# Cross-attention over 16 heads and a routed expert layer on one core: the logits move from VectorE and GpSimd to TensorE, and q, k, v travel as one record

## The chip, the cores and the metric

The kernel runs on 1 core of one Trainium2 chip. The metric is the device time of one execution in microseconds (us), taken as the median of several runs; lower is better.

## The reference

x and ctx hold 32 tiles of 128 tokens by 256 channels, in float32. The attention has 16 heads of 16 channels, and it runs over the heads of one token's q, k and v (a 16x16 table of logits for each token), not over tokens:

```python
query = (layernorm(x) @ Wq.T + bq).reshape(B, -1, H, D)      # H = D = 16
key_p = (ctx @ Wk.T + bk).reshape(B, -1, H, D)
value = (ctx @ Wv.T + bv).reshape(B, -1, H, D)
logits = einsum('bsid,bsjd->bsij', query, key_p) / sqrt(D)
out = einsum('bsij,bsjd->bsid', softmax(logits), value)
x = x + transpose(out, (0, 2, 1, 3)).reshape(B, -1, O) @ Wd.T + bd
h = layernorm(x)
gates = softmax((h @ w_red) @ normalised(wg).T); idx = argmax(gates); score = max(gates)
x = x + score * (gelu(h @ W1[idx] + b1[idx]) @ W2[idx] + b2[idx])
```

The einsum sum runs over `i, j` of one token `s`; the transpose mixes the tokens of a tile afterwards. Each token goes to one of 8 experts.

## The kernel before, in words

All five engines run hand-ordered programs that meet at semaphores. A loop index t goes from 0 to LAST; in step t each engine works on several tiles at different stages, each `live` for 32 values of t.

**Attention (t = 0 to about 36).** SyncE loads x and ctx (`sync_attention`, L238). ScalarE takes mean and variance (`moments`, L689), GpSimd raises the variance to the power -0.5 (L359), ScalarE applies it (L723), TensorE transposes and projects k and v (L864) and q (L878); biases are added by bf16 matmuls against a row of ones (L868, L875, L919). The logits are products and sums outside TensorE: `qk_mult` (L204) multiplies q by k for 16x16x16 elements of each token, 12 of the 16 rows on GpSimd in two instructions and 4 on VectorE; `qk_sum` (L212) is two reduces of 2048 elements on VectorE into PSUM. VectorE subtracts the maximum (L496, L498), ScalarE exponentiates in PSUM (L784), VectorE normalises (L467, L469, L473; its table `pr` is in PSUM). The table goes through DRAM (`a_scr`) to be laid out as blocks `aexp`, v goes through DRAM (`v_scr`) to `v2`, both in pieces of 64 bytes, and TensorE multiplies them in 16 column-tiled matmuls (L891). Then Wd and, by a matmul with the identity, x (L922, L923), the second layernorm, two transposes and the gate (L944).

**Routing.** When the first R1 = 24 tiles have their gates, `vector_early` (L516, in four parts from t = NT on) computes for them which token goes to which slot of 128 rows of one expert; S1 = 17 slots come from it. `vector_late` (L580) does the rest beside the expert work.

**Experts (39 slots).** For each slot GpSimd gathers 128 rows by an indirect DMA and scatters the result (`pool_ffn`, L376), VectorE copies the expert's W1 (`vector_up`, L663), TensorE does 4x2 and 4 accumulating matmuls, each issued as two (L995, L1020), ScalarE applies Gelu (L804), VectorE adds bias, score and residual (`vector_down`, L684). Slots 0 to 6 are issued in steps t = NT+2 = 34 to 40 beside the end of the attention, the rest in a loop of their own.

What sets the order is the written order of each engine's program: an instruction that waits holds everything behind it on its engine. In VectorE's step (L451) it is: gate maximum, 4 rows of the product, sum and normalisation of an older tile, the two reduces, maximum, subtraction.

Of the kernel before, what the change touches and what calls it, by code (L numbers as in the profile page):

```python
# [4 lines left out]
P = 128  # L5
# [12 lines left out]
ROW = 2 * C + 4  # L18
BW = 4 * C
EPS = 1e-5  # L20
HALF = NH // 2
W1W = KC * HID + KH
NB = P // NH
POOLH = 12
XR = 10
CR = 5
LAGS = 8
# [4 lines left out]
R1 = 24  # L32
WORDER = (1, 2, 0, 3)
# [5 lines left out]
LAST = NT + LAGS  # L39
FIRST = NT + 2  # L40
WARM = {NT: 4, NT + 1: 22, NT + 2: 6, NT + 3: 6}
# [4 lines left out]
SEMS = ("ld_b ld_x0 ld_x1 ld_c0 ld_c1 st_v0 st_v1 ld_v0 ld_v1 st_a0 st_a1 ld_a0 ld_a1 st_r0 st_r1 st_r2 st_r3 st_r4 ld_w0 ld_w1 ld_w2 "  # L46
        "ld_w3 ld_g ld_b1 st_b ld_br ld_moe ld_b2 pad0 bsplit filled zeroed ident ones iotas const nmax gpow wrt wrTs b1T "
        "gmm gate cat0 bpart wtr wT gsq nr2 wide xn tr_in tr_c xT cT qq kv qcp kcp vcp qk0 qk1 qks qkred0 qkred1 mx lsub "
        "exp sm rsm norm pvo oT wd x2 x2n tr_g x2T glg gm gsub score "
        "nm0 nm1 va0 va1 ve0 ve1 rs nb0 nb1 oh cnt rv selr selp selk invmm texp idg ids ig isc yo yb "  # L50
        "oh_a cnt_a rv_a selr_a selp_a selk_a invmm_a texp_a idg_a gexp8 score8 st_s "
# [3 lines left out]
def live(t):  # L55
    return 0 <= t < NT
# [6 lines left out]
def build(nc, x, ctx_in, Wq, bq, Wk, bk, Wv, bv, Wd, bd, w_red, wg, W1, b1, W2, b2, out):  # L63
# [3 lines left out]
    a_scr = nc.dram_tensor("a_scr", [NT // 2, NB, 2, NH, NH, NH], f32, kind="Internal").ap()  # L67
    v_scr = nc.dram_tensor("v_scr", [NT, P, C], f32, kind="Internal").ap()
    row_scr = nc.dram_tensor("row_scr", [NTOK, ROW], f32, kind="Internal").ap()
    bias_scr = nc.dram_tensor("bias_scr", [3, BW], bf16, kind="Internal").ap()  # L70

    es = ExitStack()
    with es:
# [9 lines left out]
        wT = sb("wT", [P, KC, 4 * C])  # L83
        brow = sb("brow", [3, BW], bf16)
        ones = sb("ones", [P, P], bf16)
        ident = sb("ident", [P, P])
        gate = sb("gate", [P, KC, NE])
# [15 lines left out]
        sc8 = sb("sc8", [P, NT - R1])  # L103
        xt = sb("xt", [P, XR, C])
# [27 lines left out]
        bT, bQ, bKV, bO, bY, bG = (bank(n) for n in ("bT", "bQ", "bKV", "bO", "bY", "bG"))  # L132
        bL = [bank("bL0"), bank("bL1")]
        wbank = (bO, bKV, bL[0], bL[1])
        lg = [t[:, 0:C].rearrange("p (i j) -> p i j", i=NH) for t in bL]
        pr = [t[:, C:2 * C].rearrange("p (i j) -> p i j", i=NH) for t in bL]

        wst = [prod[1][:, KC * w:KC * (w + 1), :] for w in range(4)]
        NR = BW // P
        bst, bres, bres2 = (sb(n, [NR, P]) for n in ("bst", "bres", "bres2"))  # L140
        bsp = sb("bsp", [NR, 3, P], bf16)
        wrp, wrT = (b2b[:, k * C:(k + 1) * C].rearrange("p (a c) -> p a c", a=KC) for k in range(2))
        wgT = sb("wgT", [NG, NE])
        wgb, wgs = (b2b[:, 2 * C + k * P:2 * C + (k + 1) * P] for k in range(2))
# [4 lines left out]
        def fl(t):  # L149
            return t[:, :, :].rearrange("p a b -> p (a b)")  # L150

        r0, r1, x0, x1 = fl(prod[0]), fl(prod[1]), fl(aexp[0]), fl(aexp[1])
# [15 lines left out]
        selr_a = [r0[:, 768 * k:768 * (k + 1)].bitcast(bf16).rearrange("p (r n) -> p r n", r=P) for k in range(2)]  # L168
# [5 lines left out]
        pos_a, limv_a, bad_a, far_a = (early(3400 + 24 * k, R1) for k in range(4))  # L174
        pint_a, pir_a, pik_a = (early(3496 + 24 * k, R1).bitcast(i32) for k in range(3))
# [4 lines left out]
        selk = [x0[:, 2048 + 640 * k:2688 + 640 * k].bitcast(bf16)[:, 0:3 * S2P * NH2]  # L180
# [18 lines left out]
        yb = [r0[:, RB * ROW + YR * C:RB * ROW + (YR + 1) * C], r1[:, 3592:3592 + C]]  # L199
        held = sb("held", [P, 2])  # L200
        rsc = [sb(f"rsc{k}", [P, 1])[:, :] for k in range(2)]
        bH = [bKV, bL[0]]

        def qk_mult(eng, t, lo, hi, q_):  # L204
            return eng.tensor_tensor(  # L205
# [32 lines left out]
        def sync_attention(eng):  # L238
            for t in range(LAST + 1):
# [33 lines left out]
                if live(e) and e % 2 == 1:  # L273
                    n = e // 2
                    for k in range(2):
                        eng.wait_ge(S[f"st_a{k}"], (n + 1) * 16)
# [812 lines left out]
```

## Time and profile before

| what | value |
|---|---|
| median of 3 runs | 472.84 us (471.21 to 474.26) |
| the profiled execution | 472.96 us, span from first to last instruction 471.1 us |
| mean granted TensorE clock | 0.964 of full speed |
| busy: TensorE, VectorE, ScalarE, GpSimd | 428.2, 359.8, 282.0, 364.7 us |

The span is 1.9 us shorter than the execution's own time. Busy time is the time in which at least one instruction of the engine is running; the groups below give the mean of one instruction, which can overlap its neighbour, so the step from one start to the next is what an engine really spends.

### The profile page before, as it was taken

How to read it: one execution, taken by the hardware profiler on the slowest of the kernel's cores; microseconds unless marked ns; L12 is line 12 of the kernel's file. 1: busy time of each engine (PE TensorE's matmuls, PEld its weight loads, DVE VectorE, ACT ScalarE, POOL GpSimd, SP SyncE). 2: the span in 40 equal slices, each digit the busy share in tenths (PEclk: the TensorE clock that was granted, in tenths of full speed). 3: DMA queues.
4: the chain of work that ended last, by engine and by line, in shares of the span. 5: the costliest groups of instructions: out<-in, count | busy, mean ns of one | idle time of the engine just before them, and what ended most of it. 6: DMA issues, size and time to landing. Idle time of an engine off the chain costs nothing.

```text
span 471.1 us, 10138 instructions
## 1 busy us (share of the span) xinstructions
PE 428.2 (91%) x3093; PEld 313.5 (67%) x3093; DVE 359.8 (76%) x583; ACT 282.0 (60%) x978; POOL 364.7 (77%) x369
## 2 busy tenths in 40 slices
PE   7877999999999999999998689798899999999990
PEld 6544555656656565656565355687799999999980
DVE  4997999999999999999999971237884565555540
ACT  4554689999999999999996324725121233322220
POOL 6999999999999999999999103345594867777731
PEclk9987999999999999999999788989999999999997
DMA  5898674787587767867666539423332333333300
GB/s 143 271 392 267 123 107 73 154 152 148 93 158 164 133 102 147 166 142 117 132 111 110 83 52 180 152 78 92 66 115 64 108 108 114 102 101 95 101 28 0
DMA packets 170283, 59.40 MB, mean 126 GB/s; under 512 B 138761, under 2 KB 160434, under 8 KB 170102
## 3 DMA queue, kind: packets, MB, share of 16 engines
q1 hardware_dynamic: 165222, 44.24, 44.5%
q0 software_dynamic: 4992, 14.51, 10.6%
q8 instruction: 26, 0.43, 0.4%
q14 instruction: 27, 0.22, 0.2%
q10 hardware_dynamic: 16, 0.00, 0.0%
HBM read 37.68 MB, written 21.96 MB: 127 GB/s over the span
## 4 chain that ended last, share of the span: by engine, by line
DVE 48%; PE 38%; issue 7%; ACT 2%; POOL 2%; DMA 1%; DVEq 1%; SPq 0%; POOLq 0%; ACTq 0%
DVE bL L213 28%; PE bQ L1020 13%; PE bKV L995 7%; DVE prod L205 7%; PE bL L995 7%; DVE mx L496 3%; DVE sm L467 2%; PE bKV L864 2%; DVE rsm L469 2%; PE bT L1004 2%; PE bQ L878 1%; DMA prod<-in_L_xattn_Wv 1%; DVE gm L460 1%; PE bO L979 1%; PE bY L922 1%
## 5 line engine op out<-in xcount | busy, mean ns | idle before, releaser
L205 POOL TENSOR_TENSOR prod<-q,kk 128x2048 f32<-128x2048 f32 x64 | 218.7, 3441 | 0.9 <-ACT q L772 0.7
L213 DVE TENSOR_REDUCE bL<-prod 128x128 f32<-128x2048 f32 x64 | 143.3, 2284 | 0.0
L1020 PE MATMUL bQ<-w,prod 128*128 x312 | 74.6, 382 | 2.9 <-DVE prod L679 2.9
L1020 PEld LDWEIGHTS bQ<-w,prod 128*128 128x128 f32 x312 | 56.3, 191 | 10.9 <-issue 4.8
L864 PE MATMUL bKV<-wT,xcT 128*128 128x512 f32 x128 | 62.6, 613 | 0.0
L804 ACT ACTIVATE prod<-bKV,prod 128x128 f32<-128x128 f32 x80 | 22.8, 368 | 56.8 <-PE bKV L995 56.8
L411 POOL DMA_INDIRECT out<-prod,isc x39 | 39.8, 1021 | 21.1 <-issue 21.1
L804 ACT ACTIVATE prod<-bL,prod 128x128 f32<-128x128 f32 x76 | 21.6, 367 | 44.5 <-PE bL L995 44.5
L359 POOL TENSOR_TENSOR rs<-ve,half 128x2 f32<-128x2 f32 x39 | 28.4, 728 | 24.5 <-ACT ve L698 22.5
L404 POOL DMA_INDIRECT prod<-row_scr,ig x39 | 40.2, 1030 | 5.8 <-issue 2.2
L679 DVE TENSOR_TENSOR prod<-bQ,b2b 128x256 f32<-128x256 f32 x39 | 16.5, 423 | 34.4 <-PE bQ L1020 33.9
L205 DVE TENSOR_TENSOR prod<-bQ,kk 128x1024 f32<-128x1024 f32 x32 | 38.9, 1214 | 3.4 <-ACT q L772 3.3
L995 PEld LDWEIGHTS bKV<-prod 128*128 128x128 f32 x320 | 39.5, 196 | 1.2 <-issue 0.4
L922 PE MATMUL bY<-wT,oT 128*128 128x256 f32 x128 | 37.9, 420 | 2.6 <-ACT oT L777 2.6
L995 PE MATMUL bKV<-prod 128*128 128x128 f32 x320 | 40.2, 280 | 0.0
L995 PEld LDWEIGHTS bL<-prod 128*128 128x128 f32 x304 | 36.6, 192 | 2.9 <-issue 2.1
L995 PE MATMUL bL<-prod 128*128 128x128 f32 x304 | 37.2, 276 | 1.2 <-DVE prod L668 1.2
L891 PE MATMUL bO<-aexp,v 128*32 128x128 f32 x1024 | 35.4, 280 | 2.9 <-DMA aexp<-a_scr 2.9
L663 DVE TENSOR_SCALAR prod<-w1b 128x1028 f32 x39 | 27.6, 707 | 13.2 <-issue 11.8
L878 PE MATMUL bQ<-wT,xcT 128*128 128x256 f32 x128 | 37.1, 413 | 0.0
L864 PEld LDWEIGHTS bKV<-wT,xcT 128*128 128x128 f32 x128 | 22.5, 196 | 16.0 <-issue 16.0
L410 POOL TENSOR_TENSOR held<-half 128x1 f32<-128x1 f32 x39 | 9.2, 237 | 30.0 <-DVE prod L684 29.8
(214 smaller groups left out, 799.6 us busy)
## 6 DMA issues: line engine op xcount, KB each, us to landing
row_scr<-cat SPq DMA_DIRECT2D x32, 258.0 KB, 4.4
xt<-in_x SPq DMA_DIRECT2D x16, 256.0 KB, 3.5
ct<-in_ctx SPq DMA_DIRECT2D x16, 256.0 KB, 3.7
v_scr<-vs SPq DMA_DIRECT2D x32, 128.0 KB, 3.0
w1b<-in_L_ffn_W SPq DMA_DIRECT2D x8, 512.0 KB, 8.7
w<-in_L_ffn_W SPq DMA_DIRECT2D x8, 512.0 KB, 8.6
a_scr<-a SPq DMA_DIRECT2D x32, 128.0 KB
v<-v_scr SPq DMA_DIRECT2D x32, 128.0 KB, 3.9
```

The lines of the kernel that those rows point to most:

```text
L205: return eng.tensor_tensor(prod[t % 2][:, lo:hi, :].rearrange("p i (j d) -> p i j d", j=NH), q_[:, lo * HD:hi * HD].rearrange("p (i d) -> ...
L213: return eng.tensor_reduce(lg[t % 2][:, h * HALF:(h + 1) * HALF, :], prod[t % 2][:, h * HALF:(h + 1) * HALF, :] .rearrange("p i (j d) -> p ...
L359: eng.tensor_tensor(rs[:, :], ve[:, :], half2[:, :], ALU.pow).then_inc(S["rs"], 1)
L404: eng.indirect_dma_start(gr[k], None, row_scr[0:R1 * P] if a < S1 else row_scr, bass.IndirectOffsetOnAxis(ap=ig[k][:, :], axis=0)).then_in ...
L411: eng.indirect_dma_start(out, bass.IndirectOffsetOnAxis(ap=isc[k][:, :], axis=0), yo[k], None, bounds_check=NTOK - 1, oob_is_err=False).th ...
L804: i_ = eng.activation(hT[a % 2][:, k, :], bH[a % 2][:, k * P:(k + 1) * P], ACT.Gelu, bias=w1s[a % 2][:, KC * HID + k:KC * HID + k + 1])
L864: eng.matmul(bKV[:, :], xcT[:, KC + k, :], wT[:, k, C:3 * C], start=(k == 0), stop=False)
L878: i_ = eng.matmul(bQ[:, 0:C], xcT[:, k, :], wT[:, k, 0:C], start=False, stop=(k == KC - 1))
L891: i_ = eng.matmul(bO[32 * r:32 * (r + 1), m * P:(m + 1) * P], v2[c % 2][:, 32 * l - 16 * s:32 * l - 16 * s + 32], aexp[c // 2 % 2][:, c % ...
L922: eng.matmul(bY[:, 0:C], oT[:, k, :], wT[:, k, 3 * C:4 * C], start=False, stop=False)
L995: i_ = eng.matmul(bH[a % 2][:, k * P:(k + 1) * P], w1s[a % 2][:, c * HID + k * P:c * HID + (k + 1) * P], gT[a % 2][:, c, :], start=(c == 0 ...
L1020: i_ = eng.matmul(bQ[:, 0:C], hT[b % 2][:, k, :], w2[:, bass.ds(eb * (KH * C) + k * C, C)], start=(k == 0), stop=(k == KH - 1))
```

## The change

The logits are now made on TensorE. VectorE writes q, k and v with their biases into one record of 16x48 floats a token, (`qkv`), which is stored to `qkv_scr` (393 KB a tile) and loaded back by heads (`ql`, in pieces of 192 bytes). GpSimd expands k to 16 blocks of 128 columns with a mask of zeros (`kx`, 2048 elements), ScalarE copies q and v into padded form (`pad`), and 16 column-tiled matmuls give the logits. The softmax table is normalised in SBUF (`pr` is now an SBUF tile), transposed by TensorE, and expanded by VectorE with the same mask (`ax`, 2048 elements). The gate's weights are multiplied into Wq and Wd in the setup, so gate logits come as 8 more columns of both projections. x is added by VectorE, bd by GpSimd. R1 is 20 and `vector_early` is in seven parts at t = 25 to 31, beside full attention steps; slots start at t = 31. The weights of the experts are loaded one transfer a step (t = 2 to 17) where before 16 transfers were issued in t = 1 and 2. The scores of the last five tiles are exponentiated after the attention loop.

```diff
-R1 = 24
+R1 = 20
-LAST = NT + LAGS
-FIRST = NT + 2
+LAST = NT + 6
+FIRST = NT - 1
+ROUTE = R1 + 5
-EXPERTS_IN = {1: range(0, NE // 2), 2: range(NE // 2, NE)}
+EXPERTS_IN = 2
...
 def pool_attention(eng):
-    for t in range(LAST + 1):
-        a, v, d = t, t - 1, t - 7
+    for t in range(-1, LAST + 1):
+        a, n, d, z = t, t + 1, t - 6, t - 2
...
+            eng.tensor_tensor(rs[t % 3][:, :], ve[:, :], half3[:, :], ALU.pow).then_inc(S["pw"], 1)
+            eng.wait_ge(S["pw"], t + 2)
+            eng.tensor_tensor(nb[t % 3][:, :], nm[:, :], rs[t % 3][:, 0:2], ALU.mult).then_inc(S["rs"], 1)
...
+        if live(z):
...
+            eng.wait_ge(S[f"ld_q{z % 2}"], (z // 2 + 1) * 16)
...
+            eng.tensor_tensor(block(kx[:, z % 2, :]), spread_heads(ql[z % 2][:, :, 0:HD]), mask_b,
+                              ALU.mult).then_inc(S["kx"], 1)
+        if live(a):
...
+            eng.tensor_tensor(xt[:, a % XR, 0:C], xt[:, a % XR, 0:C], bdb[:, :], ALU.add).then_inc(S["xb"], 1)
...
 def vector_attention(eng):
     for t in range(LAST + 1):
+        a, s0, s1, w = t, t - 3, t - 4, t - 5
...
+            # tile s0: maximum and subtraction in bL, after wait qk
+            # tile w:  cat = bY + xt (264 columns), then gate maximum
...
+            eng.tensor_tensor(block(ax[:, :]), spread_heads(bA[:, 0:C].rearrange("p (l i) -> p l i", l=NH)),
+                              mask_b, ALU.mult).then_inc(S["ax"], 1)
...
+            for k in range(2):
+                i_ = eng.tensor_tensor(qkv[a % 2][:, :, 2 * k * HD:(2 * k + 1) * HD], heads(bKV[:, k * C:(k + 1) * C], k),
+                                       heads(bqkv[:, k, :], k), ALU.add)
...
+            eng.tensor_tensor(qkv[a % 2][:, :, HD:2 * HD], heads(bQ[:, 0:C], 0), heads(bqkv[:, 2, :], 0), ALU.add)
...
+            eng.scalar_tensor_tensor(xt[:, a % XR, C:EXT], bQ[:, C:EXT], rs[(a - 1) % 3][:, 2:3], bdg[:, :],
+                                     ALU.mult, ALU.add).then_inc(S["qad"], 1)
...
+            # tile s0: sum, reciprocal, a2 = pr * rsm (both in SBUF)
+        if ROUTE <= t < ROUTE + 6:
+            vector_early(eng, t - ROUTE)
...
 def tensor_attention(eng):
...
+    # order of a step: tr_in(t) | logits blocks(t-3) | Wd(t-5), 264 columns | transpose a2(t-4)
+    #   | k,v(t), 512 columns | q(t), 264 columns | value blocks(t-4) | tr_c(t+1)
```

(The comment lines stand for code that is told here in short.) ScalarE's step is: copy of the transposed x (t), the `pad` copy (t-2, waits for the load), second layernorm and score (t-6), first layernorm (t+1), exponent (t-3), gate shift and moments (t-5), moments (t+2), copy of the values (t-4), copy of the transposed ctx (t+1). The 512 columns for k, v, the waits of each buffer and the expert slots' functions are otherwise as before.

## Rows read from the trace of the kernel before

**Rows 1.** The page: busy time of each engine, and the chain that ended last.

```profile
PE 428.2 (91%) x3093; PEld 313.5 (67%) x3093; DVE 359.8 (76%) x583; ACT 282.0 (60%) x978; POOL 364.7 (77%) x369
...
DVE 48%; PE 38%; issue 7%; ACT 2%; POOL 2%; DMA 1%; DVEq 1%; SPq 0%; POOLq 0%; ACTq 0%
```

**Rows 2.** Windows (busy PE, PEld, DVE, ACT, POOL, then clock, DMA share, GB/s).

```profile
140.00:180.00 40.00, 38.95 (x301) 23.86 (x301) 38.86 (x48) 37.37 (x136) 39.20 (x16) 1.00 0.74 141
265.00:280.00 15.00, 12.33 (x115) 7.79 (x116) 13.96 (x39) 4.54 (x16) 0.70 (x1) 0.84 0.35 57
350.00:400.00 50.00, 50.00 (x354) 47.45 (x353) 29.05 (x73) 14.02 (x50) 33.99 (x74) 1.00 0.33 98
```

**Rows 3.** Timeline of a full attention step: start us, us, engine, line, what.

```profile
160.30 0.70 POOL L359 TENSOR_TENSOR rs<-ve,half 128x2 f32<-128x2 f32 x1 [0.17 <-ACT ve L698]
160.33 0.42 DVE L496 TENSOR_REDUCE mx<-bL 128x16 f32<-128x256 f32 x1
160.48 0.44 PE L833 MATMUL bT<-ident,ct 128*128 128x128 f32 x2
...
160.78 0.43 DVE L498 TENSOR_TENSOR bL<-bL,mx 128x256 f32<-128x256 f32 x1
...
160.97 6.84 POOL L205 TENSOR_TENSOR prod<-q,kk 128x2048 f32<-128x2048 f32 x2
...
161.13 0.15 DVE L460 TENSOR_REDUCE gm<-bG 128x1 f32<-128x8 f32 x1
161.20 1.21 DVE L205 TENSOR_TENSOR prod<-bQ,kk 128x1024 f32<-128x1024 f32 x1
...
162.33 0.41 DVE L467 TENSOR_REDUCE sm<-bL 128x16 f32<-128x256 f32 x1
...
163.48 4.48 DVE L213 TENSOR_REDUCE bL<-prod 128x128 f32<-128x2048 f32 x2
163.48 1.88 PE L864 MATMUL bKV<-wT,xcT 128*128 128x512 f32 x4
163.68 0.38 ACT L744 ACTIVATE x2T<-bG 128x256 f32<-128x256 f32 x1 [0.20 <-PE bG L855]
...
165.40 0.29 ACT L698 ACTIVATE ve<-va,eps 128x1 f32<-128x1 f32 x1
...
167.13 1.08 PE L891 MATMUL bO<-aexp,v 128*32 128x128 f32 x32
```

**Rows 4.** Groups by shape, 100 to 230 us: busy, mean ns of one.

```profile
L205 POOL TENSOR_TENSOR prod<-q,kk 128x2048 f32<-128x2048 f32 x18 | 81.3, 4518 | 0.0
L922 PE MATMUL bY<-wT,oT 128*128 128x256 f32 x69 | 19.7, 406 | 0.0
L723 ACT ACTIVATE xn<-xt,nb,rs 128x256 f32<-128x256 f32 x17 | 10.2, 601 | 0.0
L692 ACT ACTIVATE junk<-xt 128x256 f32<-128x256 f32 x17 | 7.1, 418 | 0.0
```

**Rows 5.** DMA issues: KB each, median us to landing.

```profile
row_scr<-cat SPq DMA_DIRECT2D x32, 258.0 KB, 4.4
...
v_scr<-vs SPq DMA_DIRECT2D x32, 128.0 KB, 3.0
...
v<-v_scr SPq DMA_DIRECT2D x32, 128.0 KB, 3.9
```

**Rows 6.** Timeline: VectorE and GpSimd instructions that met.

```profile
9.09 3.50 POOL L340 MEMSET aexp<- 128x4096 f32 x1
...
10.10 3.57 DVE L438 CAST io_r<-io_r 128x2048 bf16<-128x2048 f32 x1
...
331.24 0.62 DVE L610 TENSOR_TENSOR aexp<-aexp,oh 128x256 f32<-128x256 f32 x1
331.33 0.58 POOL L392 COPY ig<-idg 128x1 int32<-128x1 int32 x1
```

**Rows 7.** Timeline: GpSimd's wait for the routing, and the first and last result slots.

```profile
281.25 0.19 POOL L392 COPY ig<-idg 128x1 int32<-128x1 int32 x1 [14.94 <-DVE idg L577]
...
304.92 0.48 DVE L684 SCALAR_TENSOR_TENSOR prod<-prod,rsc 128x256 f32<-128x256 f32 x1
...
460.63 0.48 DVE L684 SCALAR_TENSOR_TENSOR prod<-prod,rsc 128x256 f32<-128x256 f32 x1
...
462.00 1.00 POOL L411 DMA_INDIRECT out<-prod,isc  x1 [0.54 <-issue]
```

More of the change, by code:

```diff
@@ L615, in vector_late @@
[L615 to L623 removed]
+                after(eng.tensor_scalar(rnd, pos, (1.0 - P) / 2, ROUND, ALU.add, ALU.add))
@@ new lines, in tensor_attention @@
+                if live(a):
+                    if a > 0:
+                        eng.wait_ge(S["kvad"], a)
+                    else:
+                        eng.wait_ge(S["wT"], 2)
+                    for k in range(KC):
+                        i_ = eng.matmul(bKV[:, :], xcT[:, KC + k, :], wT[:, k, 0:2 * C], start=(k == 0),
+                                        stop=(k == KC - 1))
+                    i_.then_inc(S["kv"], 1)
+                    if a > 0:
+                        eng.wait_ge(S["qad"], a)
@@ L924, in tensor_attention @@
-                if live(d) and not live(a):
-                    tensor_gate(eng, d)
-                if t < 5:
-                    fill(eng, 10, bO)
-                if t == NT:
-                    eng.wait_ge(S["vcp"], NT)
-                    eng.wait_ge(S["wide"], 1)
-                for _ in range(WARM.get(t, 0)):
-                    eng.matmul(bKV[:, :], ones[:, :], io_r[:, 0:32, :].rearrange("p r n -> p (r n)"),
-                               start=True, stop=True)
-                if t == NT:
+                    tensor_down(eng, s)
@@ new lines, in tensor_attention @@
+                if live(s1):
+                    eng.wait_ge(S["ax"], s1 + 1)
+                    if s1 > 0:
+                        eng.wait_ge(S["oT"], s1)
+                    blocks(eng, bO, pad[:, s1 % 3, 2 * C:4 * C], ax[:, :]).then_inc(S["pvo"], 1)
+                if live(a + 1):
+                    tensor_context(eng, a + 1)
+                for s in slots:
+                    tensor_rows(eng, s)
+                if t < 4:
+                    fill(eng, 10, bA)
+                if t == ROUTE:
@@ L1025, in build @@
         rv_a, rv = [0], [0]
-        block = es.enter_context(nc.Block())
-        @block.sync
+        engines = es.enter_context(nc.Block())
+        @engines.sync
         def _(eng):
@@ L1032, in _ @@
             sync_attention(eng)
-        @block.gpsimd
+        @engines.gpsimd
         def _(eng):
@@ L1040, in _ @@
             pool_end(eng)
-        @block.vector
+        @engines.vector
         def _(eng):
@@ L1056, in _ @@
                 scalar_ffn(eng, s)
-        @block.tensor
+        @engines.tensor
         def _(eng):
```

887 lines of the change are left out of this document (413 added, 474 removed).

## The prediction

> **What bounds the kernel now.** I read the page's busy line and chain first [rows 1]: the chain is VectorE for 48% and TensorE for 38%, so there are two stages. The windows [rows 2] part them: from 140 to 180 us VectorE is busy 38.86 and GpSimd 39.20 of 40 us; from 350 to 400 us TensorE is busy all 50. Between them, 265 to 280, GpSimd works 0.70 of 15 us: it waits 14.94 us for the routing [rows 7].
> In a full attention step [rows 3] VectorE never pauses: maximum at 160.33, subtraction at 160.78 (0.45 later), gate maximum 161.13, product 161.20, sum 162.33 (1.13 later), reduces from 163.48 for 4.48 us, next maximum at 167.99. The step is 7.66 us, and 32 of them are the first stage. GpSimd is nearly as full: 6.84 for two products, 0.7 for the power. The last stage is 155.7 us from slot 0's result (304.92) to slot 38's (460.63), then 10.5 us to the end of the span [rows 7]; the diff leaves its work per slot alone.
>
> **The new attention step, engine by engine** (start to start, from [rows 3, 4]).
> VectorE loses the two reduces (4.48) and the 1024-element product (1.13). It gains the expansion, 2048 elements: the 1024-element product's step is 1.13, of which 0.07 is fixed (161.13 to 161.20 for a tiny one), so 2.20; four adds of some 256 elements at 0.35 (the step behind the subtraction) and one of 8 at 0.1. With maximum 0.45, subtraction 0.35, residual add and gate maximum 0.46+0.07, sum, reciprocal and a2 0.45+0.36+0.34: I take one residual add, three adds into the record, and get 5.8 us. Call M the start of the maximum; the expansion starts at M+1.33, the record is ready at M+4.7, a2 starts at M+5.5 and ends at M+5.9.
> GpSimd: power 0.70, a small multiply about 0.2, k's expansion 4.52 (the same 2048 elements of two inputs [rows 4]; bounds 4.5 and, were it at the pair's 6.84 for 3072 elements, 4.6), bd about 0.74 (a quarter of 2.1 us per 1024 plus 0.2). Sum 6.2.
> TensorE: three pairs of transposes at 0.37, k and v 1.71, q and Wd 0.89 each (four matmuls of 264 columns, 0.216 of step each), two sets of blocks at 1.01 (L891, from 167.13 to the next start). Sum 6.6. It drops the bias rows, the identity matmul and the gate's four. But the ctx transposes, now last in the step, must be copied by ScalarE before the next step's transposes may start. A copy starts 0.47 after its transposes do (163.21 to 163.68), takes 0.38, and 0.08 leads back: 0.94 in place of 0.37. TensorE's loop is 7.17 us. The loop through the logits, VectorE and the value blocks is as long: 0.37+1.16+1.33+2.28+0.05+1.01+0.94 = 7.14.
> ScalarE: two moments of 1.45 (a 0.418 activation, its accumulator, a second pair, ve), two layernorm applications 0.51 each, copies at 0.29, the pad copy of 512 elements 0.56 (bounds 0.5 and 1.0: once or twice L723's 0.51), scores 0.5; with its own wait for TensorE 6.9 us.
> DMA: M is 1.5 us into the step (0.37+1.16), so the record is ready at 6.2. The store of 393 KB is bounded by 3.0 and 6.6 (128 KB took 3.0, 258 KB 4.4 [rows 5]; one and a half times the latter); I take 4.7, as fixed latency is a large part of it. The load, 2048 pieces of 192 bytes, is bounded by 3.9 (as many pieces of 64) and 6; I take 4.7. It lands 15.7 us after (with 0.1 for the issue) its step began, and `pad` wants it two steps on. From there ScalarE's rest of the step is 6.2: three steps in 15.7+6.2 = 21.9 us, 7.3 each. So four resources lie between 6.9 and 7.3; I take 7.3 (bounds 6.9 and 7.9), 0.36 less than 7.66.
>
> **Where the two elementwise engines meet.** A rival price is inside the profile [rows 6]: VectorE's cast began at 10.10 while GpSimd's memset ran from 9.09 to 12.59, and lasted to 13.67, where 2048 elements need about 1.1 after 12.59. And GpSimd's copy of one element, begun 0.09 after a VectorE multiply with both inputs in SBUF, took 0.58 in place of 0.19 and ended 0.05 after it. So the two wait for each other for a whole instruction. In the kernel before, every VectorE instruction beside the 6.8 us of GpSimd products has a PSUM input. After the change a2 reads two SBUF tiles, and so do most of the routing's instructions, which now stand in steps 25 to 30 beside k's expansion. The Trainium skill, "SBUF — State Buffer", section "Who interferes with whom", says the same: a VectorE instruction with two SBUF inputs and a GpSimd one that reads SBUF exclude each other, and the later one blocks fully. The trace agrees (0.58 against 0.19); without that rule and those rows the forecast would be the first rival's.
> When does k's expansion start? The power waits for ScalarE's moments: exponent at M+0.92 at the earliest, shift M+1.45, moments of 1.47 twice, to M+4.6, then 0.1+0.78+0.2: M+5.66, not 0.2 after a2 has started. In a normal step the load lands later (rel. M+6.8). So a2 passes first, and the plain steps pay nothing.
> Routing: its parts take 1.1 to 2.1 us each by the same instructions of the kernel before and follow a2. Part 0 (step 25) fits before k's expansion. The other five meet it: from M+5.9 VectorE stands until M+10.3, then finishes 1.4 to 2.1 us of routing: 12.1 us a step in place of 7.3. Without exclusion such a step would be 5.8+2 = 7.8.
>
> **The sum.** Record 0 is ready at 13.5 (setup as long as before: k, v of tile 0 at about 11), stored 18.0, loaded 22.7, expanded 27.4, its logits at 28.6 = M of step 3. Then 23 steps of 7.3: 196.5 = M of step 26. Five steps of 12.1: 257. Step 30 ends with 20 small matmuls of the inversion which wait for the last selection, in front of the next step's transposes: +2, 259. Steps 31 and 32: no q, k, v work, but GpSimd's power now waits for one moment only, so k's expansion starts at M+4.2, before a2, and holds it to M+8.7; with the first W1 copy 9.1 and 10.6. Step 33, 7.0; result of slot 0 some 6.5 into step 34: 292.2. In the kernel before this was 304.92, of which 15 us were GpSimd's wait; that wait goes. From there the stage of 39 slots as before, 155.7, and 10.5: span 458.4, and with 1.9 outside it 460.3 us, against 472.96 of the profiled execution and the median 472.84, which are the same within 0.1%. Saved are some 7 us in plain steps and 26 between step 31 and the first result (33 in place of 59, by the step of 7.66 counted back from the last one); some 26 are paid back in steps 26 to 30, and the rest is in the first steps, where the weights' transfers no longer stand in one block.
> Costed at nothing: the setup's products with Wq and Wd (TensorE waits for weights there; uncovered, 2 us), the weights' transfers in steps 2 to 17 (the DMA share was 0.74 with 4096 pieces of 64 bytes a tile, now 2048; uncovered, about 1 us a step, 16 us), the table loads between Gelu and exponent (1.3 us each, hidden under TensorE). The granted clock is 1.00 in a full step and 0.84 from 265 to 280 us [rows 2], where TensorE was busy 12.3 of 15. In the blocked steps TensorE has 6.6 us of work at full clock in 12; at the lower level it would still fit.
>
> **The rivals.**
> 1. No exclusion in the routing steps, since the routing's instructions pass between. For it: part 0 does. Against: rows 6, and 4.5 us of expansion in each step. Steps of 7.8: 22 less; steps 31 and 32 5 less: 434 us. Chance 0.22.
> 2. The exclusion locks in. If k's expansion starts before a2 in plain steps too (0.2 us decide, at M+5.66 against M+5.5), a2 ends 4.5 later and the next step starts so: 10.6 us a step. ScalarE is then ahead, so it repeats itself. 22 plain steps of 3.3 more: 533 us. For it: any long step brings the load in early. Against: the order at the margin, and that the load is late in plain steps. Chance 0.10, slower.
> 3. The trip through DRAM is longer, 12 us and more beside the weights' transfers: steps of 8.1 to 8.3, 478 to 483 us. For it: a store of 393 KB, twice the 64-byte pieces' bytes. Chance 0.10.
> The forecast has 0.58.
>
> **How the numbers follow.** The forecast's own spread is 9 us (0.4 on 23 steps). The measurement can tell about 1% from no change. Below 468.1 lie 0.85 of the forecast and rival 1: 0.70 for faster. Within 1%: 0.08 of the forecast and a little of rival 3, 0.10. Slower 0.20. The range, 431 to 484, takes in rivals 1 and 3 and leaves out the lock.
>
> **What would show it.** Attention steps of 7.3 us with VectorE busy under 6 of them; a2 at its plain 0.4 us in plain steps; in steps 26 to 30 a routing instruction with a duration of 3 to 4.5 us beside k's expansion, and steps of 12 us; first slot's result near 292; 3.73 us a slot at the end. Wrong it is if a2 lasts over 4 us in plain steps (rival 2), if no routing instruction is long (rival 1), or if GpSimd and ScalarE wait for the load for over 1 us a step (rival 3).

## The result, and the profile after

The changed kernel takes 494.12 us (median of 4 runs, 493.2 to 498.86) against 473.55 us for the kernel before (471.21 to 475.87) in the same comparison: a ratio of 1.0455, 95% interval 1.0368 to 1.0541. It is slower. The forecast was 460 us, with 431 to 484 as its range; the result lies outside. The prediction's own rival 2 (chance 0.10) is there, in a milder form, but it is not the whole of it: of the 34 us between forecast and measurement it holds about 10, and without it the kernel is still slower than before (e1, e2). The profiled execution has a span of 493.0 us.

I read the page first: busy line, chain, three groups and three transfers (columns of the groups: engine, operation, tiles, count, busy us, mean ns, idle before).

```profile
PE 404.7 (82%) x3785; PEld 308.1 (62%) x3785; DVE 351.2 (71%) x664; ACT 253.3 (51%) x835; POOL 302.2 (61%) x407
...
PE 40%; DVE 24%; DMA 16%; issue 11%; ACT 5%; SPq 2%; DVEq 1%; POOL 0%; ACTq 0%; POOLq 0%
...
L344 POOL TENSOR_TENSOR kx<-ql,mask 128x2048 f32<-128x2048 f32 x32 | 117.5, 3673 | 25.9 <-issue 22.8
L329 POOL TENSOR_TENSOR rs<-ve,half 128x3 f32<-128x3 f32 x39 | 34.8, 892 | 90.6 <-ACT ve L682 90.6
...
L492 DVE TENSOR_TENSOR a<-pr,rsm 128x256 f32<-128x256 f32 x32 | 56.5, 1766 | 3.6 <-DVE rsm L488 0.5
...
qkv_scr<-qkv SPq DMA_DIRECT2D x32, 384.0 KB, 3.9
ql<-qkv_scr SPq DMA_DIRECT2D x32, 384.0 KB, 4.7
```

Against [rows 1] GpSimd and VectorE gave up 62.5 and 8.6 us of busy time, and the kernel still got slower. The chain, which was VectorE for 48% and TensorE for 38%, now has 16% DMA: the wait for the record is visible in it. The row to stop at is a2 (L492): 32 instructions of 256 elements with a mean of 1766 ns, where the same form takes 590 ns when nothing holds it (the timelines below). A mean of this kind hides two populations, so I looked at stretches and at single steps. The windows (busy PE, PEld, DVE, ACT, POOL, then clock, DMA share, GB/s):

```profile
84.00:145.00 61.00, 54.45 (x657) 35.14 (x656) 50.33 (x97) 49.15 (x169) 43.34 (x33) 1.00 0.89 240
190.00:226.00 36.00, 23.44 (x285) 14.36 (x283) 35.24 (x44) 21.99 (x73) 21.70 (x16) 1.00 0.51 141
221.00:226.00 5.00, 0.57 (x10) 0.20 (x2) 4.86 (x5) 0.72 (x2) 4.92 (x4) 0.99 0.50 164
226.00:231.00 5.00, 3.40 (x37) 2.37 (x38) 1.78 (x5) 2.17 (x7) 0.65 (x1) 0.50 0.34 47
360.00:480.00 120.00, 119.10 (x810) 111.99 (x809) 67.85 (x163) 34.30 (x120) 79.69 (x176) 0.97 0.32 92
```

From 84 to 145 us VectorE is busy for 50.33 of 61 us, the DMA engines for 0.89 (0.74 in [rows 2]). From 190 to 226 us VectorE is busy 35.24 of 36 again, though no work was added and the DMA load has fallen. The slot stage (360 to 480) is as it was. The granted clock is 1.00 from 190 to 226 us, so TensorE's clock does not lengthen these steps. I call a step locked when a2 stands in it until k's expansion is through. One such step, 206.88 to 216.46, in the timeline (start us, us, engine, line, what):

```profile
211.41 0.86 POOL L329 TENSOR_TENSOR rs<-ve,half 128x3 f32<-128x3 f32 x1 [3.91 <-ACT ve L682]
...
212.50 3.67 POOL L344 TENSOR_TENSOR kx<-ql,mask 128x2048 f32<-128x2048 f32 x1
212.66 3.88 DVE L492 TENSOR_TENSOR a<-pr,rsm 128x256 f32<-128x256 f32 x1
...
216.46 0.41 DVE L435 TENSOR_REDUCE mx<-bL 128x16 f32<-128x256 f32 x1
...
216.59 0.44 PE L858 MATMUL bA<-ident,a 128*128 128x128 f32 x2 [1.60 <-DVE a L492]
...
217.37 0.38 ACT L735 ACTIVATE pr<-bL 128x256 f32<-128x256 f32 x1 [2.03 <-DVE bL L437]
...
219.99 0.91 DVE L464 TENSOR_TENSOR qkv<-bKV,bqkv 128x256 f32<-128x256 f32 x2
...
220.82 0.58 DVE L475 TENSOR_TENSOR qkv<-bQ,bqkv 128x256 f32<-128x256 f32 x1
...
221.32 0.22 DVE L479 SCALAR_TENSOR_TENSOR xt<-bQ,rs,bdg 128x8 f32<-128x8 f32 x1
```

k's expansion starts 0.16 before a2, and a2 ends 0.37 after it. The next maximum, TensorE's transposes of a2 (1.60 idle) and ScalarE's exponent (2.03 idle) all wait for that one instruction. Then GpSimd waits 3.91 for ScalarE and both meet again 9.58 us later, 222.08 against 222.25. Nothing pulls them apart: the late a2 delays everything by the same amount. In the routing steps of this kernel the instruction that is held is again a2 (3.86 to 3.88 us in steps 26 to 29, for example at 237.74), and none of the routing's own, which run behind it and take 1.30 us at most:

```profile
237.74 3.88 DVE L492 TENSOR_TENSOR a<-pr,rsm 128x256 f32<-128x256 f32 x1
```

In a plain step under the weights' transfers the order is the other one, since the record has not landed (idle before k's expansion 1.97, and `pad` shows what it is: the load):

```profile
119.86 0.59 DVE L492 TENSOR_TENSOR a<-pr,rsm 128x256 f32<-128x256 f32 x1
...
121.66 0.63 ACT L708 ACTIVATE pad<-ql 128x512 f32<-128x512 f32 x1 [1.14 <-DMA ql<-qkv_scr]
121.71 3.68 POOL L344 TENSOR_TENSOR kx<-ql,mask 128x2048 f32<-128x2048 f32 x1 [1.97 <-issue]
```

The starts of the maximum (M) divide the loss. "M of 3" is the start in step 3, "3->20" the time from step 3's to step 20's, all in us and each from one profiled execution; the last column runs from M of step 31 to the last slot's result.

```
                      M of 3   3->20   20->25  25->26  26->31  M of 31  31->last slot
predicted               28.6   124.1     36.5     7.3    62.5    259.0     188.9
after                  36.07   131.5     48.9    14.2    61.0    291.6     190.8
after, once more       36.68   136.0     48.5    14.2    60.8    296.2     191.1
e1 rsm in PSUM         37.09   137.2     38.4    13.9    57.9    284.4     190.6
e2 wait for a2         37.90   137.5     40.6    13.8    62.5    292.4     186.3
e3 waits a2, routing   35.60   135.8     41.1     9.7    44.3    266.5     185.0
e4 weights spread only 36.84   150.9     48.3    14.2    60.8    311.2     189.4
e5 e3, weights spread  36.16   128.2     39.1    10.3    43.3    257.1     187.0
e6 setup               34.89   125.0     41.7     9.7    43.0    254.3     186.5
e7 order of TensorE    35.38   123.9     36.5    10.1    44.4    250.2     186.7
e8 rsm in PSUM again   33.92   123.8     42.1     9.7    43.0    252.5     192.6
e9 bias table only     37.28   139.6     47.9    14.2    60.4    299.5     188.2
e10 bias table late    35.93   121.5     34.8     9.7    43.1    245.0     186.4
```

Of 32.6 us at step 31, 7.5 are the start, 7.4 plain steps, 12.4 lie between steps 20 and 25 (four locked steps of 9.6 to 10.2, and before them one of 9.9, which is not locked: the bias table's transfer lies in it, e10), and 6.9 in the step from 25 to 26, the first routing step; the five steps behind it came out at 61.0 where 62.5 were forecast. Another 1.9 us are lost behind step 31. The four locked steps hold 9.8 us more than four of 7.3.

### The profile page after: what moved, and what is told of

The parts are those of the page before. It is cut to its first block, busy times and chain, and to the rows that moved or that the text cites. A ratio compares the mean times of both kernels' runs of the same rounds, so it can differ in the third digit from the quotient of the medians.

```text
span 493.0 us, 11383 instructions
## 1 busy us (share of the span) xinstructions
PE 404.7 (82%) x3785; PEld 308.1 (62%) x3785; DVE 351.2 (71%) x664; ACT 253.3 (51%) x835; POOL 302.2 (61%) x407
## 3 DMA queue, kind: packets, MB, share of 16 engines
q0 software_dynamic: 4992, 14.61, 10.2%
## 4 chain that ended last, share of the span: by engine, by line
PE 40%; DVE 24%; DMA 16%; issue 11%; ACT 5%; SPq 2%; DVEq 1%; POOL 0%; ACTq 0%; POOLq 0%
PE bQ L995 13%; DMA qkv_scr<-qkv 9%; DVE a L492 7%; PE bKV L962 7%; PE bX L962 6%; DMA ql<-qkv_scr 5%; PE bY L851 3%; PE bL L822 3%; DVE ax L455 3%; DVE qkv L464 2%; DVE cat L444 2%; PE bT L977 2%; DMA bdc<-in_L_xattn_bd 1%; SPq L256 1%; DVE qkv L475 1%
## 5 line engine op out<-in xcount | busy, mean ns | idle before, releaser
L344 POOL TENSOR_TENSOR kx<-ql,mask 128x2048 f32<-128x2048 f32 x32 | 117.5, 3673 | 25.9 <-issue 22.8
L995 PE MATMUL bQ<-w,wA 128*128 x312 | 74.6, 382 | 3.2 <-DVE r L662 3.1
L455 DVE TENSOR_TENSOR ax<-bA,mask 128x2048 f32<-128x2048 f32 x32 | 73.3, 2290 | 0.0
L995 PEld LDWEIGHTS bQ<-w,wA 128*128 128x128 f32 x312 | 56.6, 192 | 10.5 <-issue 4.3
L866 PE MATMUL bKV<-wA,xcT 128*128 128x512 f32 x128 | 62.1, 608 | 0.0
L492 DVE TENSOR_TENSOR a<-pr,rsm 128x256 f32<-128x256 f32 x32 | 56.5, 1766 | 3.6 <-DVE rsm L488 0.5
L388 POOL DMA_INDIRECT out<-r,isc x39 | 40.5, 1039 | 22.1 <-issue 22.1
L381 POOL DMA_INDIRECT r<-row_scr,ig x39 | 40.2, 1031 | 6.1 <-issue 2.2
L851 PE MATMUL bY<-wD,oT 128*128 128x264 f32 x128 | 40.6, 444 | 0.5 <-ACT oT L749 0.5
L822 PE MATMUL bL<-kx,pad 128*32 128x128 f32 x1024 | 39.6, 302 | 0.5 <-POOL kx L344 0.5
L962 PEld LDWEIGHTS bX<-wA,r 128*128 128x128 f32 x304 | 38.4, 199 | 1.5 <-issue 0.6
L435 DVE TENSOR_REDUCE mx<-bL 128x16 f32<-128x256 f32 x32 | 13.5, 421 | 31.8 <-PE bL L822 31.7
```

The lines of the kernel that those rows point to most:

```text
L344: eng.tensor_tensor(block(kx[:, z % 2, :]), spread_heads(ql[z % 2][:, :, 0:HD]), mask_b, ALU.mult).then_inc(S["kx"], 1)
L381: eng.indirect_dma_start(gr[k], None, row_scr[0:R1 * P] if a < S1 else row_scr, bass.IndirectOffsetOnAxis(ap=ig[k][:, :], axis=0)).then_in ...
L388: eng.indirect_dma_start(out, bass.IndirectOffsetOnAxis(ap=isc[k][:, :], axis=0), yo[k], None, bounds_check=NTOK - 1, oob_is_err=False).th ...
L455: eng.tensor_tensor(block(ax[:, :]), spread_heads(bA[:, 0:C].rearrange("p (l i) -> p l i", l=NH)), mask_b, ALU.mult).then_inc(S["ax"], 1)
L492: eng.tensor_tensor(a2[s0 % 2][:, :].rearrange("p (m j b) -> p m j b", m=KC, j=NH), p.rearrange("p (m b j) -> p m j b", m=KC, b=NB), rsm[: ...
L822: i_ = eng.matmul(out_[32 * r:32 * (r + 1), m * P:(m + 1) * P], stat[:, 32 * l - 16 * s:32 * l - 16 * s + 32], moving[:, l * P:(l + 1) * P ...
```

## The experiments

The theory after the first comparison: exclusion between a2 (two SBUF inputs) and k's expansion costs 2.2 us in each plain step in which the record is on time, and the same exclusion makes routing steps of 12 us. Rivals: TensorE's clock, or the DMA trip, as the cause.

**e1: one input of a2 moved into PSUM.** Nothing waits; a2 only has one SBUF input in place of two.

```diff
-        rsm = sb("rsm", [P, NH])
+        rsm = bQ[:, 480:480 + NH]
```

(with a wait for the last a2 before the expert stage uses the bank.)

> The changed kernel with the reciprocal of the sum in PSUM (16 unused columns of q's bank), so that a2's multiply has one SBUF input and not two. Theory (exclusion between a two-SBUF-input VectorE instruction and GpSimd's expansion of k): a2 lasts about 0.6 us in every step, steps 21 to 25 fall from 9.6 to about 7.6 us, the routing steps 26 to 30 stay near 11.5 since the routing's own instructions still have two SBUF inputs; 494 becomes about 479 us. Rival (a2 is long for a reason of its own, its strided read of SBUF or a slow spell): the long steps stay, 494 us.

Measured 487.21 us, ratio 1.0304 (1.024 to 1.0367). Timeline of e1:

```profile
211.21 3.67 POOL L344 TENSOR_TENSOR kx<-ql,mask 128x2048 f32<-128x2048 f32 x1
211.37 0.59 DVE L492 TENSOR_TENSOR a<-pr,bQ 128x256 f32<-128x256 f32 x1
...
212.69 0.42 DVE L435 TENSOR_REDUCE mx<-bL 128x16 f32<-128x256 f32 x1 [0.72 <-PE bL L822]
```

The same overlap with the same 0.16 us between the starts, and a2 lasts 0.59 in place of 3.88. Steps 20 to 25 take 38.4 us in place of 48.9, four of them 7.39 to 7.40. This is the cleanest proof of the exclusion: neither order nor load was changed. The time fell by 7 us and not by the 15 expected: the plain steps were longer in this execution (137.2 against 131.5; e5 and the repeat bear on that), and the start by 1.0. With the lock gone the kernel is still 3% slower than before.

**e2 and e3: k's expansion waits.** e2 makes GpSimd wait for a2; e3 has that and, in steps 26 to 31, also a wait for the last VectorE instruction of the routing's part.

```diff
+                    if z > 1:
+                        eng.wait_ge(S["norm"], z - 1)
+                    done = {0: ("oh_a", 1), 1: ("rv_a", 8), 2: ("rv_a", 13), 3: ("texp_a", 1), 4: ("selk_a", 1),
+                            5: ("taken_a", 1)}.get(t - 1 - ROUTE)
+                    if done:
+                        eng.wait_ge(S[done[0]], done[1])
                     eng.tensor_tensor(block(kx[:, z % 2, :]), spread_heads(ql[z % 2][:, :, 0:HD]), mask_b,
...
```

(e2 has the first two lines only.)

> The changed kernel, with one wait more: GpSimd's expansion of k waits until a2 of the step before is written. Theory (exclusion, decided by who starts first): a2 lasts 0.6 us everywhere, k's expansion starts some 0.6 us later, which nobody notices; the same gain as with the reciprocal in PSUM, about 479 us; some of the routing's instructions are still held for up to 3.7 us. Rival (the steps from 21 on are long for want of something else, and a2 only shows it): a wait more can only cost, 494 us or above.

> As the run with the wait for a2, and in steps 26 to 31 k's expansion also waits for the last instruction of the routing's part of the step before. Theory: no VectorE instruction meets k's expansion, the routing steps fall from 11.5 to about 8.5 us, 15 us more gained, about 464 us, below the kernel before. Rival (routing steps are long because of their own work): as the run with the wait for a2 alone, about 479 us.

Measured: e2 487.35 us (479 expected; the profiled execution took 490.97), ratio 1.0287 (1.0212 to 1.0362); e3 463.97 us, ratio 0.9799 (0.9731 to 0.9866), all against the same runs of before. What e2 leaves, in its timeline, and what e3 makes of it, in its own:

```profile
237.66 3.67 POOL L346 TENSOR_TENSOR kx<-ql,mask 128x2048 f32<-128x2048 f32 x1 [0.87 <-DVE a L494]
237.92 3.60 DVE L533 SCALAR_TENSOR_TENSOR r<-r,io_m 128x160 f32<-128x160 f32 x1
```

```profile
203.72 0.59 DVE L498 TENSOR_TENSOR a<-pr,rsm 128x256 f32<-128x256 f32 x1
...
204.48 3.68 POOL L350 TENSOR_TENSOR kx<-ql,mask 128x2048 f32<-128x2048 f32 x1 [0.88 <-DVE a L498]
...
230.22 0.32 DVE L537 SCALAR_TENSOR_TENSOR r<-r,io_m 128x160 f32<-128x160 f32 x1
...
247.80 0.17 DVE L558 TENSOR_SCALAR texp<-r 128x13 int32<-128x13 f32 x1
...
247.88 0.41 DVE L441 TENSOR_REDUCE mx<-bL 128x16 f32<-128x256 f32 x1
...
248.15 3.67 POOL L350 TENSOR_TENSOR kx<-ql,mask 128x2048 f32<-128x2048 f32 x1 [2.67 <-DVE texp L558]
```

In e2 a2 is free (0.58) and the next instruction with two SBUF inputs is held in its place: 3.60 us for 160 elements that take 0.32 in e3 (230.22). In e3 GpSimd waits 0.88 us for a2 in a plain step and 2.67 for the routing at 248.15, the steps are no longer for it, and the expansion lies beside the maximum and the products that read PSUM. Steps 26 to 31 take 44.3 us in place of 61.0, and the first routing step 9.7 in place of 14.2. In the windows of after, that step shows why it is dearer than the others: from 221 to 226 us TensorE is busy for 0.57 of 5 us, since a2 and then the routing's one-hot table (which expert each token goes to, as zeros and ones) keep it waiting, and from 226 to 231 its granted clock is 0.50, the lower of its two levels (1.2 in place of 2.4 GHz). The 32 blocks of the logits then took 1.94 us, not 1.08, and Wd's product 2.13, not 1.16:

```profile
228.69 1.94 PE L822 MATMUL bL<-kx,pad 128*32 128x128 f32 x32
230.56 2.13 PE L851 MATMUL bY<-wD,oT 128*128 128x264 f32 x4
```

So two kinds of semaphore wait turn 4.5% slower into 2% faster. That e3 is within 1 us of its forecast of 464 is partly luck: e2 came out 8 us above its own 479, and the waits in the routing steps brought 23 us where 15 were put.

**e4: the weights' transfers spread, without any wait.** If the late record is what keeps the lock out of steps 3 to 20, then a lighter DMA load must make the kernel slower.

```diff
-                n = t - EXPERTS_IN
+                n = t // 2 if t >= 0 and t % 2 == 0 else -1
```

> The changed kernel with the 16 transfers of the experts' weights in every second step (0 to 30) in place of steps 2 to 17; nothing else. Theory (the record's load comes late in steps 4 to 20 only because the weights' transfers lie beside it, and that lateness keeps k's expansion behind a2): with the load early the exclusion begins some 15 steps sooner, those steps go from 7.7 to 9.6 us, and the kernel gets slower, about 515 to 525 us. Rival (weights' transfers only cost): plain steps fall by up to 0.4 us, about 487 us.

Measured 512.75 us, 504.19 to 515.84 (before 472.74); in its profile (the execution of 512.78 us):

```profile
99.99 3.67 POOL L344 TENSOR_TENSOR kx<-ql,mask 128x2048 f32<-128x2048 f32 x1
100.16 3.87 DVE L492 TENSOR_TENSOR a<-pr,rsm 128x256 f32<-128x256 f32 x1
```

a2 is long from step 7 on (at 71.12, 4.01 us), and of the steps up to 25 only one has it short (186.77). With half the transfers a step the kernel loses more time. The medians are 18.6 us apart against the first measurement of the changed kernel and 14.0 against the second (498.77), the fastest run of e4 only 10.1 and 5.4; but all four of its runs lie above all eight of that kernel (at most 500.18). In the traces steps 3 to 20 take 150.9 us, against 131.5 and 136.0. The sign was a forecast of the mechanism; a theory in which the transfers only cost has the other sign. What makes one run of e4 8 us faster than the rest is not shown: only one execution has a trace.

**e5: the same spreading under the two waits of e3.**

> Both waits of e3 (k's expansion after a2, and after the routing's VectorE instructions), and the expert weights' sixteen 512 KB transfers issued in every second step from 0 to 30 in place of each of steps 2 to 17. Theory (the 0.35 to 0.6 us a step by which steps 3 to 20 are longer than the 7.39 us of steps 22 to 25 is the record's trip through DRAM beside one 512 KB transfer a step, share of the DMA engines 0.86): with half the load a step it mostly hides; steps 3 to 20 take 7.4 to 7.6 us, the maximum of step 20 comes 6 to 10 us earlier than in e3: 454 to 458 us. Rival (it is a constant of the step, of ScalarE or of the clock, not of the transfers): 463 to 465, no change. Second rival (each transfer costs its own time wherever it stands, two queues' worth behind each other): steps with a transfer of 8 us and steps without of 7.4, sum the same, 462 to 464.

Measured 455.47 us, ratio 0.9618 (0.9567 to 0.9669). From step 6 to step 20, fourteen in a row take 7.38 to 7.40 us. So the 0.3 to 0.7 us by which plain steps were longer in after and e1 to e3 are the record's trip beside the weights' transfers, as rival 3 had it in small. The same edit makes the kernel slower without the waits (e4) and brings 8.5 us with them.

**e6: the setup's bias column.** Its copy and its semaphore leave the head of VectorE's queue.

```diff
-            eng.tensor_copy(bdm, bdc[:, :].unsqueeze(2).broadcast_to((P, KC, P))).then_inc(S["bdm"], 1)
...
+            eng.wait_ge(S["ld_bc"], 16)
+            eng.tensor_copy(bdm, bdc[:, :].unsqueeze(2).broadcast_to((P, KC, P))).then_inc(S["bdm"], 1)
```

> e5, and the setup's copy of Wd's bias column, whose transfer of small elements landed 7.4 us after its issue and kept VectorE idle until 10.7 us, gets a semaphore of its own and moves behind VectorE's other setup work. Theory (the first records wait for VectorE's setup): maximum of step 3 at 31 to 33 us in place of 36, so 3 to 5 us less than e5. Rival (the first steps wait for TensorE's products of Wq and Wd or for the weights): no change, within 1 us.

Measured 453.41 us, ratio 0.9573 (0.953 to 0.9616), 2 us less than e5, where 3 to 5 were expected; the two intervals overlap. The first VectorE instruction of the setup, in after and in e6:

```profile
10.69 0.29 DVE L405 TENSOR_TENSOR b2b<-b2b 128x128 f32<-128x128 f32 x1 [10.69 <-DMA bdc<-in_L_xattn_bd]
```

```profile
9.54 0.29 DVE L411 TENSOR_TENSOR b2b<-b2b 128x128 f32<-128x128 f32 x1 [9.54 <-DMA wgT<-in_L_ffn_wg]
```

It starts at 9.54 (11.95 in e5), now behind the next small-element transfer, but M of step 3 moves by only 1.3 us, to 34.89, where 31 to 33 was expected. It also varies without the edit: 35.60 to 37.90 in the eight profiles with the old setup, 33.92 to 35.93 in the four with the new one. Neither theory is right as put: the bias column was late and in the way by 1 to 2 us.

**e7: TensorE's order.** The transposes of the next ctx go ahead of the value blocks, their copy ahead of the values' copy on ScalarE.

```diff
+                if live(a + 1):
+                    tensor_context(eng, a + 1)
                 if live(s1):
                     eng.wait_ge(S["ax"], s1 + 1)
...
-                if live(a + 1):
-                    tensor_context(eng, a + 1)
```

> e6, and TensorE's transposes of the next ctx stand ahead of the value blocks, ScalarE's copy of them ahead of the copy of the values. Theory (an undisturbed step of 7.39 us is TensorE's chain: ctx transposes last in the step, 0.47 until ScalarE's copy starts, 0.4 of copy, 0.07 back, before the next step's transposes): the copy now hides beside the value blocks, and a step becomes 6.8 to 7.1 us where the record's trip permits (three steps in its 21 to 22 us): 5 to 10 us less than e6, 444 to 452 us. Rival (the record's trip or ScalarE sets 7.39): no change against e6. Second rival (the copy of ctx now holds up ScalarE ahead of the exponent): 3 us more.

Measured 450.75 us, ratio 0.9555 (0.9496 to 0.9614): 2.7 us less than e6, where 5 to 10 were expected, and the two intervals overlap, so that the times alone do not show a gain. Which wait ends last, 100 to 145 us, in e6 and then in e7 (us in total, times, longest):

```profile
PEld bT L842 <- ACT xcT L763: 4.3, 6, 0.7
...
POOL kx L350 <- DMA ql<-qkv_scr: 1.0, 1, 1.0
```

```profile
PEld bT L842 <- ACT xcT L756: 4.7, 6, 1.8
...
ACT pad L715 <- DMA ql<-qkv_scr: 3.5, 5, 1.7
```

The steps are now 6.58 to 8.26 us, no longer even: some run at 6.58, which the old order never reached, and in others ScalarE waits up to 1.7 us for the record's load. The mean of steps 3 to 20 falls only from 7.35 to 7.29. The ctx loop was the bound of the 7.39 us step, and the record's trip stands right behind it. The prediction had three steps in no less than 21.9 us; from step 6 on the shortest three in a row took 20.5 (steps 15 to 17), and three steps of the mean are 21.9.

**e8: e6 with rsm in PSUM in place of the wait for a2.**

> e6 without the wait of k's expansion for a2; in its place the reciprocals stand in PSUM, so that a2 reads only one SBUF tile. Theory (two-SBUF-input exclusion alone made the lock, and the wait costs nothing since k's expansion has slack): the same as e6 within 2 us, and a2 at 0.59 us throughout although it overlaps k's expansion. Rival (the wait makes k's expansion late in each step and is itself part of the 7.4 us): 3 to 8 us less than e6.

Measured 455.38 us, ratio 0.9614 (0.9577 to 0.9651), 2 us more than e6, as expected within 2; the intervals overlap. Steps 7.39 and a2 at 592 ns on average, as in e6 (596): the wait does not lengthen a plain step, k's expansion has slack. The profiled executions are 4.2 us apart (457.37 and 453.14), and that is lost at the end of the attention: up to M of step 31 e8 is 1.8 us ahead, and the first slot's result came 11.4 us after the last maximum, 7.4 in e6. Why was not followed.

**e9: the bias table's transfer moved, without waits.** The lock of after began behind a 9.9 us step, in which this 1 MB transfer lies. Is the long step its cause?

```diff
-                if t == EXPERTS_IN + 2 * NE:
+                if t == 31:
```

> The kernel after the change with one transfer moved: the 1 MB expert bias table is issued in step 31 in place of step 18. Question: what starts the lock at step 21? Theory (the record's load being on time is enough; an undisturbed step has k's expansion at M+5.6 to M+5.95 and a2 at M+5.8 to M+6.07, so k's expansion is first in any step whose load has landed, and it is late in steps 2 to 20 only because of the weights' transfers): without the long step 20 the lock still comes once the weights are through, at step 19 to 21, and the steps to 25 stay at 9.6 us; the time falls only by the 2 us of the long step or not at all, 490 to 494 us. Rival (the 10 us step behind the bias table's transfer is what brings the load in early): steps of 7.4 us up to step 25, 12 to 14 us less than after, 480 us.

Two of its four runs took 498.0 and 499.93 us, the others 517.17 and 517.76 (before 474.61); the profiled one took 499.93, and what makes the other two slower has no trace. Timeline:

```profile
166.53 3.68 POOL L344 TENSOR_TENSOR kx<-ql,mask 128x2048 f32<-128x2048 f32 x1 [0.62 <-issue]
166.61 0.42 DVE L435 TENSOR_REDUCE mx<-bL 128x16 f32<-128x256 f32 x1 [1.65 <-PE bL L822]
...
172.95 3.66 POOL L344 TENSOR_TENSOR kx<-ql,mask 128x2048 f32<-128x2048 f32 x1
173.03 3.96 DVE L492 TENSOR_TENSOR a<-pr,rsm 128x256 f32<-128x256 f32 x1 [0.46 <-DVE rsm L488]
```

The lock comes without the long step, and two steps sooner (step 19; the last weights' transfer is issued in step 17): in this execution the first record that lands in time is enough. The time was missed: 490 to 494 was put against the 494 us of another chip, and the unaltered kernel took 498.77 beside it.

**e10: e7 with the bias table in step 31.**

> e7 with the 1 MB bias table issued in step 31. Theory (the 9.5 to 10.6 us step 19 to 20 of e5 to e8 is the record waiting behind this transfer): that step falls to 7, the time by 3 to 5 us against e7, 446 to 448 us. Rival (the first expert weights or the clock make that step): no change, 450 to 451.

Measured 445.38 us, ratio 0.941 (0.9364 to 0.9456). Steps 19 and 20 take 8.5 and 7.0 us in place of 10.4 and 8.5. The medians of e7 and e10 are 5.4 us apart, on two chips; 3.4 of them lie in these two steps. This is the fastest version, 29 us less than before (474.61 beside it). Its page:

```profile
PE 388.0 (88%) x3785; PEld 305.2 (69%) x3785; DVE 313.1 (71%) x664; ACT 250.8 (57%) x835; POOL 300.7 (68%) x407
```

VectorE's busy time is 38.1 us less than after's with the same 664 instructions, and 37.5 of it is a2 (56.5 us of busy time there, 19.0 here): that much was waiting, counted as work.

**The changed kernel once more**, on the chip of e9 and e10.

> The kernel after the change once more, unaltered, beside the others of this call. Theory (the 7.7 to 8.1 us of plain steps in after, e1, e2 and e3 differ by chance of how the DMA transfers fall, not by the edits): 492 to 497 us, maxima of steps 3 to 20 between 131 and 138 us apart, in place of 131.5 in the first profile; the lock again from step 20 or 21 on, with a2 at 3.9 us. Rival (the edits of e1 to e3 lengthen plain steps by 0.3 us): 131 to 132 us again.

Measured 498.77 us, ratio 1.0495 (1.0435 to 1.0554), 1.8 above the expected band. Steps 3 to 20 took 136.0 us here and 131.5 in the first profile of the same code, so the 137.2 of e1 need not be an effect of its edit. The lock started at step 21 again, with a2 at 3.87.

## Why the prediction was wrong, by its steps

The profiled execution took 494.8 us where 460.3 were forecast, 34.5 more. By the table this is 7.5 for the start, 7.4 for plain steps up to step 20, 2.6 for step 20, 9.8 for the lock, 6.9 for the first routing step, 1.5 less in the other routing steps, and 1.9 behind step 31. So two kinds of step failed: an order that was argued from a margin, and terms that were put at nothing.

- **"a2 passes first, and the plain steps pay nothing."** This step failed, and its failure is the lock, 9.8 us. It set a2 at M+5.5 and k's expansion at M+5.66. The expansion was right: M+5.62 in the locked step (206.88 to 212.50), and in an undisturbed step of e3 (maximum at 197.65) GpSimd was free for it at 203.60, M+5.95. a2 was not: M+5.78 in the locked step and M+6.07 (203.72) in the undisturbed one. So k's expansion is first in both, whenever its record is there. The record's adds were priced at 1.15 us and take 1.46 (0.91 + 0.58 + 0.22, from 219.99 to the next instruction at 221.45); in undisturbed steps the expansion of the transposed a2 (`ax`) starts at M+1.6, as it stands behind a wait for Wd's product, not M+1.33. An error of 0.3 to 0.6 us in a sum of durations turned the sign of a margin of 0.16. The prediction named the margin ("0.2 us decide") and gave the other side 0.10. With terms read to 0.1 us or worse, that was a toss of a coin at best.
- **"The load is late in a normal step."** True for most of steps 3 to 20, and for the wrong reason: the weights' transfers, costed at nothing, made it late. e4 and e9 show that the load is on time without them. The term that was mis-sized is the store, put at 4.7 us: beside the weights' transfers it took 4.7 (84 to 145 us), in the quiet stretch from 190 to 226 us 2.5. In e3's undisturbed step the store was issued at 203.03 and the load at 205.47, and with the 4.9 us that a load takes there it lands at about 210.4, M+5.3 of the next step and not M+6.8 (an estimate from these rows). The two lines are those of after, 84 to 145 us, and then 190 to 226:

```profile
qkv_scr<-qkv SPq DMA_DIRECT2D x8, 384.0 KB, 4.7
```

```profile
qkv_scr<-qkv SPq DMA_DIRECT2D x4, 384.0 KB, 2.5
```

The cost that was left out hid the cost that had been found.
- **The price of the lock.** Rival 2 said 10.6 us a step; 9.58 was measured, 2.2 over 7.39 in place of 3.3. k's expansion takes 3.67 us and not the 4.52 of [rows 4]. And it began only at step 21, which is why the time is 494 and not 533; in e4 it holds 18 steps.
- **Plain step of 7.3 us: right.** Undisturbed steps take 7.39. The loop through the logits had 7.14; its maximum-to-product term is 1.6 in place of 1.33, and 7.14 + 0.27 is 7.41. The copy of ctx (0.94 predicted, 0.91 from 202.61 to 203.52 in e3) was right, and so was the load (4.7). The 7.73 of after is that step plus the weights' transfers, which were put at nothing: the text said up to 16 us uncovered; against 17 steps of 7.39 it was 5.9 in the first profile and 10.4 in the second. The 1 MB bias table's transfer was in no term; it made the 9.9 us of step 20.
- **Routing steps of 12.1 us: right in size, by another instruction.** They took 11.4 to 12.7 and 13.5, sum 61.0 against 62.5. The prediction let a2 pass and the routing's instruction be held, 3 to 4.5 us long; in the kernel as changed it is a2 that is held, and a held routing instruction is seen only in e1 and e2, where a2 is free (3.60 at 237.92). Whichever is held, the wait ends with k's expansion, so the step comes out nearly the same; that is luck as far as the order goes. By the Trainium skill, "SBUF — State Buffer", section "Who interferes with whom", a VectorE instruction with two SBUF inputs and a GpSimd instruction that reads SBUF exclude each other for the whole instruction; the trace agrees, 3.88 against 0.59 with one input moved to PSUM. Rival 1 is out. What failed is part 0, in step 25, which was to fit before k's expansion. It stands behind a2, which k's expansion has already passed, so it is late too; with a2 free (e1, e2) the step is as long, 13.9 and 13.8 us, and only the wait for the routing makes it 9.7. So 4.5 of the 6.9 us are the exclusion, and 2.4 remain although nothing is held: part 0's own work was put at nothing too. TensorE, idle meanwhile in after, then runs at the lower granted clock for 5 us; "at the lower level it would still fit" costed that at nothing, and the blocks and Wd's product alone became 1.8 us longer.
- **The start: 7.5 us late.** Record 0 was to be ready at 13.5 and its store was issued at 23.06. The first transposes start at 16.1, where k and v of tile 0 were put at 11. Setup was not as long as before, and its products with Wd, put at nothing, are not hidden (beside Wq the gate's weights stand as columns of their own; only Wd is multiplied, L912). They stand on TensorE from 20.30 to 21.9, behind the first tile's q (19.41), and VectorE's add of q waits for their results until 22.30, with record 0 behind it:

```profile
20.67 1.04 PE L912 MATMUL bY<-wA,kx 128*128 128x8 f32 x8
...
21.92 0.17 DVE L469 COPY bdg<-bY 128x8 f32<-128x8 f32 x1 [1.38 <-PE bY L914]
...
22.30 0.59 DVE L475 TENSOR_TENSOR qkv<-bQ,bqkv 128x256 f32<-128x256 f32 x1
```

  The bias column is 1.3 us of the late start in the two profiles compared (e6); the rest was not taken apart by a run.
- **The last stage: right within 2.8 us.** From the first slot's result (324.00) to the last (482.48) 158.5 us, predicted 155.7; 10.5 us from there to the end.

## What to carry to other kernels

Where VectorE and GpSimd both work from SBUF, list the VectorE instructions with two SBUF inputs and write down by a wait which side goes first; here a wait of 0.9 us on the engine with slack took 3.3 us off an instruction of the one without, and 2.2 us off the step. A margin of a few tenths of a microsecond is not a safe order, above all where the state that a miss makes repeats itself: price the locked state and give it an even chance. And an edit that is good in itself (less DMA load) can be judged only once such a lock is gone: it made the kernel slower without the waits (e4) and brought 8.5 us with them.

## What the runs showed that I had not expected

- A time that is worse with less traffic in each step: 512.75 us with the weights spread, medians of 494 and 499 with one transfer in every step.
- k's expansion, 2048 elements of GpSimd with the mask repeated from a small tile and k strided, takes 3.67 us; the product of that size in the kernel before, whose q and k are both repeated too but lie dense in the innermost 16 elements, took 4.52 [rows 4]. Which difference of the operands makes it is not shown.
- A busy share that is a wait. In the locked stretch VectorE shows 35.24 of 36 us busy; the blocked time is inside the instruction's duration, not in the idle column. The sign is one group's mean (1766 ns) beside the same form's 590 in steps that are not locked.
- Steps beside the weights' transfers vary from one execution to the next: the same kernel took 131.5 and 136.0 us for the same 17 steps in two executions, on two chips.
